# Two convolution stages of a fused image kernel run as one pipeline, dwc's convolution five blocks behind cpe1's

## Chip, cores and metric

The kernel runs on one core of a Trainium2 chip. The metric is the device time of one execution in microseconds (us), 3555.57 us as the median of three runs (3555.01 to 3556.33).

## What is computed

Four images of 128 channels by 96 x 96 go through four layers, all in float32 but the last convolution. The layers before and after (a patchwise filter, a selective scan, attention, an MLP, a binary convolution) are not touched. What the change moves is the head of the third layer:

```python
t = t + img2tok(_dwconv(tok2img(t), cpe1_w, cpe1_b))
shortcut = t
tn = _ln(t, n1_g, n1_b)
act_res = jax.nn.silu(tn @ actproj_w + actproj_b)
ti = tn @ inproj_w + inproj_b
ti = jax.nn.silu(img2tok(_dwconv(tok2img(ti), dwc_w, dwc_b)))
ta = _attn(ti, Hh, Ww, qk_w, qk_b, lepe_w, lepe_b)
```

`_dwconv` is a depthwise 3 x 3 convolution, `_ln` a normalisation over the 128 channels.

## The kernel before

Channels lie on the 128 partitions. An image is cut into NB = 12 blocks of 8 rows (768 columns), and each stage works block by block in one of four large regions `R[0]` to `R[3]`, with small double-buffered tiles in `work` and the eight banks of PSUM. Nothing is scheduled by a tool. For each engine the program writes out its instructions by `overlapped` (L71): a run is a start step and a list of (lag, stage), and at step t a stage of lag l in a run of start s is emitted for block t - s - l, in the order of the lists. Engines are joined by counting semaphores: `a.wait_ge(e1["var"], done(i, b))` waits for block b of image i. The order of a list is therefore the order of execution on its engine, and an instruction that waits holds up all behind it.

The head of the layer is two stages, one after the other, in `middle(i)` of each engine:

- **cpe1** (`cpe1_run`, start NB + 1, beside the last steps of the scan's normalisation `norm_run`). ScalarE writes the centre tap (`cpe1_centre`, L878), VectorE adds the left and right taps (`side_tap`, L1502), TensorE convolves the other six taps from row-shifted copies (`convolve`, L1128, by `shifted_taps`, L1033), VectorE adds the two (`add_taps`, L1487). Then the normalisation: TensorE subtracts the mean (`centre`), ScalarE squares (L865), TensorE averages (`var`), ScalarE takes Ln and Exp (`root`, L869, L871), VectorE multiplies (`normalise`, L1492). All products of TensorE go by `product` (L1013).
- **dwc** (`dwc_run`, start 2 NB + 4). TensorE multiplies by `w_in` and `w_act` (`in_act`, L1150), VectorE writes `ti` (L1513), ScalarE the Silu of the other (`silu_act`, L885). `dwc` convolves `ti` six blocks later in the same way (centre L896, taps L1502, sum L1520), and `silu_v` (L889) writes the result.

Then follow the keys of the attention (start 3 NB + 7): `stage` copies a block (L906), `keys` turns and multiplies it (L1176, L1177), `key_in` (L1533), `key_exp` (L914 to L918), `key_phi`, `key_turned` (L1548), `kv_sum` (L1193).

The row-shifted copies come by DRAM. SP's queue stores each finished block (`store_x` L554, `store_ti` L567) into a scratch, and fetches it in four DMAs (`fetch_shifted`, L536) into one of two halves of a buffer, `shifted_rows(p)`, p = b % 2, once the block after it has landed there and the convolution of block b - 2 is done. cpe1 and dwc both use both halves, dwc after cpe1:

```python
pipelined(sp, NB, [(3, load_x_shifted), (0, store_x)])
pipelined(sp, NB, [(3, load_ti_shifted), (0, store_ti)])
```

[...]

## Time and profile before

| | us |
|---|---|
| median of 3 runs | 3555.57 |
| profiled execution | 3555.76 |
| span of its trace | 3554.0 |
| TensorE busy | 2939.3 (83%) |
| VectorE busy | 2377.0 (67%) |
| ScalarE busy | 2255.9 (63%) |
| GpSimd busy | 1105.1 (31%) |

The span runs from the first to the last instruction. Busy shares are means over stages of different kinds, and say nothing of one stage. In a timeline a row is an instruction, or several of one line merged (x48), with its start, the time from its start to the end of the last, and in brackets the idle time of its engine before it with what ended it. Two instructions of one engine overlap at their ends by about 0.1 us. On TensorE a float32 matmul counts as two, so that a `product` of two halves is x4. [...]

### The profile page before, as it was taken

How to read it: one execution, taken by the hardware profiler on the slowest of the kernel's cores; microseconds unless marked ns; L12 is line 12 of the kernel's file. 1: busy time of each engine (PE TensorE's matmuls, PEld its weight loads, DVE VectorE, ACT ScalarE, POOL GpSimd, SP SyncE). 2: the span in 40 equal slices, each digit the busy share in tenths (PEclk: the TensorE clock that was granted, in tenths of full speed). 3: DMA queues.
4: the chain of work that ended last, by engine and by line, in shares of the span. 5: the costliest groups of instructions: out<-in, count | busy, mean ns of one | idle time of the engine just before them, and what ended most of it. 6: DMA issues, size and time to landing. Idle time of an engine off the chain costs nothing. (4 is left out here: it accounts for less than half of the span.)

```text
span 3554.0 us, 45053 instructions
## 1 busy us (share of the span) xinstructions
PE 2939.3 (83%) x17500; PEld 1601.4 (45%) x17500; DVE 2377.0 (67%) x2469; ACT 2255.9 (63%) x2485; POOL 1105.1 (31%) x612
## 2 busy tenths in 40 slices
PE   3688876979979877788997988777988788769799
PEld 2344335545535434444553543443555444354355
DVE  5777656875478646687457964768736876576861
ACT  2877545568687645447778774644868876454584
POOL 0246003642025500373103630146300462025530
...
GB/s 69 18 1 41 124 220 100 171 9 0 71 27 1 59 140 212 109 135 9 0 90 9 1 105 125 201 135 90 9 13 86 0 5 151 146 174 135 46 0 54
...
## 3 DMA queue, kind: packets, MB, share of 16 engines
...
q8 instruction: 141, 2.31, 0.3%
...
## 5 line engine op out<-in xcount | busy, mean ns | idle before, releaser
L1502 DVE SCALAR_TENSOR_TENSOR work<-region,cols,work 128x768 f32<-128x768 f32 x288 | 373.8, 1298 | 8.4 <-ACT work L896 3.3
L677 POOL TENSOR_TENSOR region<-region 128x768 f32<-128x768 f32 x96 | 230.9, 2407 | 322.2 <-ACT region L856 315.6
L1013 PE MATMUL psum<-region,m_fc 128*128 128x384 f32 x768 | 286.4, 496 | 11.1 <-ACT work L963 11.1
L1278 PE MATMUL psum<-work,m_fc 128*128 128x384 f32 x768 | 282.7, 492 | 0.0
L1013 PE MATMUL psum<-region,m_cen 128*128 128x384 f32 x384 | 162.6, 549 | 112.4 <-DVE region L1617 45.3
L220 DVE SCALAR_TENSOR_TENSOR region<-region,cols 128x768 f32<-128x768 f32 x192 | 239.8, 1249 | 4.0
L641 POOL TENSOR_TENSOR work<-work 128x768 f32<-128x768 f32 x48 | 99.4, 2074 | 439.8 <-ACT work L780 425.2
L653 POOL TENSOR_TENSOR work<-work,region 128x768 f32<-128x768 f32 x96 | 174.0, 1812 | 193.8 <-ACT work L795 193.8
L963 ACT ACTIVATE work<-psum,cols 128x768 f32<-128x768 f32 x192 | 173.0, 901 | 90.9 <-PE psum L1013 86.2
L1013 PE MATMUL psum<-work,m_avg 128*128 128x384 f32 x576 | 217.3, 500 | 15.1 <-ACT work L818 7.2
L1424 DVE SCALAR_TENSOR_TENSOR work<-region,cols,work 128x768 f32<-128x768 f32 x144 | 195.9, 1381 | 39.4 <-POOL work L641 36.0
L1013 PEld LDWEIGHTS psum<-region,m_fc 128*128 128x128 f32 x768 | 145.8, 194 | 123.5 <-ACT work L963 33.4
L692 POOL COPY region<-work 128x768 f32<-128x768 f32 x4 | 3.3, 826 | 634.9 <-DVE work L1539 634.9
L927 ACT ACTIVATE region<-psum,cols 128x768 f32<-128x768 f32 x48 | 43.2, 901 | 235.5 <-PE psum L1013 235.5
L1278 PEld LDWEIGHTS psum<-work,m_fc 128*128 128x128 f32 x768 | 142.9, 191 | 110.5 <-DVE region L1621 19.2
L1013 PEld LDWEIGHTS psum<-region,m_cen 128*128 128x128 f32 x384 | 70.2, 203 | 203.6 <-issue 113.8
L1445 DVE TENSOR_TENSOR_SCAN work<-work,psum 128x768 f32<-128x768 f32 x88 | 159.7, 1814 | 3.1
L1621 DVE SCALAR_TENSOR_TENSOR region<-psum,cols,region 128x768 f32<-128x768 f32 x48 | 48.9, 1018 | 165.8 <-PE psum L1278 165.8
L1013 PE MATMUL psum<-region,m_w_dt 128*128 128x384 f32 x384 | 146.3, 505 | 16.0 <-issue 10.3
L1013 PEld LDWEIGHTS psum<-work,m_avg 128*128 128x128 f32 x576 | 107.7, 193 | 108.8 <-ACT work L818 30.3
L704 POOL TENSOR_TENSOR region<-work,region 128x768 f32<-128x768 f32 x48 | 90.9, 1893 | 208.9 <-DVE work L1587 208.9
L669 POOL TENSOR_TENSOR region<-work,region 64x768 f32<-64x768 f32 x48 | 115.4, 2405 | 124.9 <-DVE work L1471 124.9
...
## 6 DMA issues: line engine op xcount, KB each, us to landing
...
```

The lines of the kernel that those rows point to most:

```text
L220: eng.scalar_tensor_tensor(out=tgt, in0=prow(k, b, *TAPS[n]), scalar=tap_weight(conv, TAPS[n]), in1=tgt, op0=ALU.mult, op1=ALU.add).then_i ...
L641: g.tensor_tensor(tile(4 + p), tile(p), tile(2 + p), ALU.add).then_inc(b_taps[0], 1)
L653: g.tensor_tensor(tile(2 + p), tile(p), flat(2, sweep_block(sweep, b)), ALU.mult).then_inc(c["du"], 1)
L669: g.tensor_tensor(flat(1, b)[0:CM], tile(2 + p)[CM:P], flat(1, b)[CM:P], ALU.mult).then_inc(d_gate, 1)
L677: g.tensor_tensor(chain_tile(conv, n, p), chain_tile(conv, n - 1, p), chain_tile(conv, n, p), ALU.add).then_inc(tap_done[n], 1)
L704: g.tensor_tensor(region_tile(3, 4 + p), tile(p), region_tile(3, 2 * p), ALU.mult).then_inc(f2_qc, 1)
L963: a.activation(halves(tile(4 + j)), pair(0), ACT.Gelu, bias=col("fc1_o", j)).then_inc(g_gelu, 1)
L1013: last = pe.matmul(psum[:, bank + s, 0:HC], weights[:, :], moving(s), start=(n == 0), stop=(n == len(terms) - 1))
L1278: last = pe.matmul(psum[:, 4 + s, 0:HC], fc2[:, P * j:P * (j + 1)], static(tile(4 + j))(s), start=(j == 0), stop=(j == 3))
L1424: v.scalar_tensor_tensor(out=by_row(tile(6 + p)) if n == 4 else sofar, in0=prow(3, b, *scan_tap(n)), scalar=col("l1taps", n), in1=sofar, o ...
L1445: v.tensor_tensor_scan(way(tile(6 + p)), way(tile(4 + p)), way(bu_flat[p]), initial=start, op0=ALU.mult, op1=ALU.add).then_inc(c["h"], 1)
L1502: v.scalar_tensor_tensor(out=by_row(tile(acc + p)), in0=prow(k, b, *TAPS[n]), scalar=tap_weight(conv, TAPS[n]), in1=by_row(tile(acc + p)), ...
```

## The change

cpe1 and dwc become one run, `local_run`, on each of the three engines. On TensorE it starts at NB + 1, on ScalarE and VectorE at NB + 2; dwc's convolution has lag 6 where cpe1's has 1. `in_act` is split into `to_in` and `to_act`, which use one pair of banks in turn. PSUM is shared out anew: cpe1's convolution and `var` in banks 0 and 1 (so `convolve` now waits for the Ln of the block before), `centre` in 2 and 3 without a second buffer, in and act in 4 and 5, dwc's convolution in 6 and 7. dwc's tiles move to `tile(4 + p)`. The keys' run starts at 2 NB + 3 on TensorE and 2 NB + 4 on the others. `root` and `silu_v` load their tables ahead of their waits. The two halves of the shifted rows are shared: cpe1 has both for its first five blocks (`FRESH`) and then half 0, dwc has half 1 and for its last four blocks both; a load into a half used alone waits for the convolution of block b - 1. SP's list is one, in which a load of dwc's last four blocks stands ahead of the store of its step and cpe1's load of block 2 ahead of the last store of cpe1.

```diff
 
...
 
+        def x_half(b):
+
+            return b % 2 if isinstance(b, int) and b < FRESH else 0
+
+        def ti_half(b):
+
+            return b % 2 if isinstance(b, int) and b >= NB - FRESH else 1
...
                 def load_x_shifted(b, p):
                     rows_landed(x_stored, b, p)
-                    sp.wait_ge(e1["conv"], done(i, b - 2))
-                    fetch_shifted("cpe1", b, p, x_shifted[p])
+                    sp.wait_ge(e1["conv"], done(i, b - 2 if b < FRESH else b - 1))
+                    fetch_shifted("cpe1", b, x_half(b), x_shifted[p])
...
                 def load_ti_shifted(b, p):
                     rows_landed(ti_stored, b, p)
-                    if is_first(b):
+                    if b == 0:
+                        sp.wait_ge(e1["conv"], done(i, FRESH - 2))
+                        sp.sem_inc(rows_seen, 1)
+                    if ti_half(b) == 0:
                         sp.wait_ge(e1["conv"], done(i, NB - 1))
-                        sp.sem_inc(rows_seen, 1)
-                    sp.wait_ge(e2_conv, done(i, b - 2))
-                    fetch_shifted("dwc", b, p, ti_shifted[p])
+                    sp.wait_ge(e2_conv, done(i, b - 2 if b > NB - FRESH else b - 1))
+                    fetch_shifted("dwc", b, ti_half(b), ti_shifted[p])
...
-                pipelined(sp, NB, [(3, load_x_shifted), (0, store_x)])
-                pipelined(sp, NB, [(3, load_ti_shifted), (0, store_ti)])
+                for b in range(NB):
+                    if b == NB - 1:
+                        load_x_shifted(2, 0)
+                    store_x(b, b % 2)
+                    if 3 <= b < 5:
+                        load_x_shifted(b - 3, (b - 3) % 2)
+                pipelined(sp, NB, [(0, lambda b, p: load_x_shifted(b, p) if 2 < b < FRESH else None),
+                                   (5, lambda b, p: load_ti_shifted(b, p) if b > NB - FRESH else None),
+                                   (3, store_ti),
+                                   (5, lambda b, p: load_ti_shifted(b, p) if b <= NB - FRESH else None),
+                                   (0, lambda b, p: load_x_shifted(b, p) if b >= FRESH else None)])
...
                 def root(b, p):
+                    a.preload_act_table_set("natural_log_exp_and_others")
                     a.wait_ge(e1["var"], done(i, b))
-                    a.activation(halves(tile(2 + p)), pair(6), ACT.Ln, bias=col("eps")).then_inc(e1["log"], 1)
...
-                cpe1_run = [(0, cpe1_centre), (3, squares), (4, root)]
...
                 def silu_act(b, p):
                     a.wait_ge(e2_mm, done(i, b))
-                    a.activation(halves(flat(2, b)), pair(2), ACT.Silu, bias=col("act_o")).then_inc(e2_act, 1)
+                    a.activation(halves(flat(2, b)), pair(4), ACT.Silu, bias=col("act_o")).then_inc(e2_act, 1)
 
                 def silu_v(b, p):
+                    a.preload_act_table_set("silu_and_others")
                     a.wait_ge(e2_sum, done(i, b))
-                    a.activation(prow(0, b), by_row(tile(2 + p)), ACT.Silu).then_inc(e2_v, 1)
...
                 def dwc_centre(b, p):
                     if is_first(b):
                         a.wait_ge(borders, i * 5 + 4)
                     a.wait_ge(e2_ti, done(i, b))
-                    a.wait_ge(e2_sum, done(i, b - 2))
-                    a.activation(by_row(tile(p)), prow(3, b), ACT.Identity, scale=tap_weight("dwc", TAPS[0]),
+                    a.wait_ge(e2_v, done(i, b - 2))
+                    a.activation(by_row(tile(4 + p)), prow(3, b), ACT.Identity, scale=tap_weight("dwc", TAPS[0]),
                                  bias=col("dwc_b")).then_inc(e2_centre, 1)
 
-                dwc_run = [(0, silu_act), (5, dwc_centre), (7, silu_v)]
+                local_run = [(2, squares), (0, cpe1_centre), (2, root), (6, silu_v), (5, dwc_centre), (3, silu_act)]
...
-                overlapped(a, NB, [(0, norm_run), (NB + 1, cpe1_run), (2 * NB + 4, dwc_run),
-                                   (3 * NB + 7, [(0, stage), (2, key_exp)])])
+                overlapped(a, NB, [(0, norm_run), (NB + 2, local_run), (2 * NB + 4, [(0, stage), (2, key_exp)])])
...
                     pe.wait_ge(e1["t"], done(i, b - 1))
+                    pe.wait_ge(e1["log"], done(i, b - 1))
...
-                    shifted_taps("cpe1", 0, p, True).then_inc(e1["conv"], 1)
+                    shifted_taps("cpe1", 0, x_half(b), True).then_inc(e1["conv"], 1)
...
                 def centre(b, p):
+                    if is_first(b):
+                        pe.wait_ge(d_norm, done(i, NB - 1))
                     pe.wait_ge(e1["t"], done(i, b))
-                    pe.wait_ge(e1["tn"], done(i, b - 2))
-                    product(2 + 2 * p, [(cen128, image_rows(1, b))]).then_inc(e1["yc"], 1)
+                    pe.wait_ge(e1["tn"], done(i, b - 1))
+                    product(2, [(cen128, image_rows(1, b))]).then_inc(e1["yc"], 1)
 
                 def var(b, p):
+                    pe.wait_ge(e1["sq"], done(i, b))
+                    product(0, [(avg128, static(tile(2 + p)))]).then_inc(e1["var"], 1)
+
+                def to_in(b, p):
+                    if is_first(b):
+                        pe.wait_ge(d_log, done(i, NB - 1))
+                    pe.wait_ge(e1["tn"], done(i, b))
+                    pe.wait_ge(e2_act, done(i, b - 1))
+                    product(4, [(w_in, flat_rows(2, b))]).then_inc(e2_in, 1)
+
+                def to_act(b, p):
+                    pe.wait_ge(e2_ti, done(i, b))
+                    product(4, [(w_act, flat_rows(2, b))]).then_inc(e2_mm, 1)
+
+                def dwc(b, p):
                     if is_first(b):
                         pe.wait_ge(d_out, done(i, NB - 1))
-                    pe.wait_ge(e1["sq"], done(i, b))
-                    pe.wait_ge(e1["log"], done(i, b - 1))
-                    product(6, [(avg128, static(tile(2 + p)))]).then_inc(e1["var"], 1)
-
-                cpe1_run = [(3, centre), (4, var), (1, convolve)]
-
-                def in_act(b, p):
-                    if isinstance(b, int) and b < 2:
-                        pe.wait_ge(e1["tn"], done(i, NB - 2 + b))
-                    pe.wait_ge(e2_ti, done(i, b - 1))
-                    pe.wait_ge(e2_act, done(i, b - 1))
-                    product(0, [(w_in, flat_rows(2, b))])
-                    product(2, [(w_act, flat_rows(2, b))]).then_inc(e2_mm, 1)
-
-                def dwc(b, p):
                     pe.wait_ge(ti_shifted[p], i * (32 * NB) + (b * 32 + (64 - 32 * p)))
-                    pe.wait_ge(e2_sum, done(i, b - 2))
+                    pe.wait_ge(e2_sum, done(i, b - 1))
                     pe.sem_inc(shift_begun, 1)
-                    shifted_taps("dwc", 4 + 2 * p, p, True).then_inc(e2_conv, 1)
-
-                dwc_run = [(0, in_act), (6, dwc)]
+                    shifted_taps("dwc", 6, ti_half(b), True).then_inc(e2_conv, 1)
+
...
```

VectorE's lists, which the cut leaves out, become `local_run = [(6, dwc_left), (6, dwc_right), (3, ti), (0, cpe1_left), (0, cpe1_right), (2, normalise), (6, dwc_sum), (1, cpe1_sum)]`, start NB + 2.

TensorE, the passage from cpe1 to dwc before (`m_cen` is centre, `m_avg` var, `m_w_in` and `m_w_act` in_act, `m_cpe_shifted` the convolution):

```order
L1033 MATMUL psum<-work,m_cpe_shifted 32x384 x24
L1013 MATMUL psum<-region,m_cen 128x384 x2
L1013 MATMUL psum<-work,m_avg 128x384 x2
L1013 MATMUL psum<-region,m_cen 128x384 x2
L1013 MATMUL psum<-work,m_avg 128x384 x4
L1013 MATMUL psum<-region,m_w_in 128x384 x2
L1013 MATMUL psum<-region,m_w_act 128x384 x2
```

and one full step of it now:

```order
L1034 MATMUL psum<-region,m_cen 128x384 x2
L1034 MATMUL psum<-region,m_w_in 128x384 x2
L1034 MATMUL psum<-work,m_avg 128x384 x2
L1054 MATMUL psum<-work,m_dwc_shifted 32x384 x24
L1054 MATMUL psum<-work,m_cpe_shifted 32x384 x24
L1034 MATMUL psum<-region,m_w_act 128x384 x2
```

All six kinds of work stand in one step, cpe1's convolution right behind dwc's.

ScalarE, the same passage before (L871 Exp, L885 silu_act, L896 dwc_centre, L889 silu_v):

```order
L871 ACTIVATE work<-work 128x768
L885 ACT_TABLE_LOAD
L885 ACTIVATE region<-psum,cols 128x768 x6
L896 ACTIVATE work<-region,cols 128x768
L885 ACTIVATE region<-psum,cols 128x768
L896 ACTIVATE work<-region,cols 128x768
L885 ACTIVATE region<-psum,cols 128x768
L896 ACTIVATE work<-region,cols 128x768
L889 ACTIVATE region<-work 128x8x96
```

and one full step now (L886 squares, L900 cpe1_centre, L891 Ln, L893 Exp, L911 silu_v, L918 dwc_centre, L906 silu_act):

```order
L886 ACTIVATE work<-psum 128x768
L900 ACTIVATE work<-region,cols 128x768
L889 ACT_TABLE_LOAD
L891 ACTIVATE work<-psum,cols 128x768
L893 ACTIVATE work<-work 128x768
L909 ACT_TABLE_LOAD
L911 ACTIVATE region<-work 128x8x96
L918 ACTIVATE work<-region,cols 128x768
L906 ACTIVATE region<-psum,cols 128x768
```

A table load that stood once between the stages now stands twice in each step.

TensorE at the end of dwc, before (L1176 and L1177 are `keys`):

```order
L1033 MATMUL psum<-work,m_dwc_shifted 32x384 x24
L1013 MATMUL psum<-region,m_w_in 128x384 x2
L1013 MATMUL psum<-region,m_w_act 128x384 x2
L1033 MATMUL psum<-work,m_dwc_shifted 32x384 x144
L1176 MATMUL psum<-m_w_k,region 128x128
L1177 MATMUL psum<-m_ident,region 128x128
```

and now (L1201 and L1202 are `keys`):

```order
L1034 MATMUL psum<-work,m_avg 128x384 x2
L1054 MATMUL psum<-work,m_dwc_shifted 32x384 x24
L1034 MATMUL psum<-region,m_w_act 128x384 x2
L1034 MATMUL psum<-region,m_w_in 128x384 x2
L1054 MATMUL psum<-work,m_dwc_shifted 32x384 x24
L1034 MATMUL psum<-region,m_w_act 128x384 x2
L1054 MATMUL psum<-work,m_dwc_shifted 32x384 x24
L1201 MATMUL psum<-m_w_k,region 128x128
L1202 MATMUL psum<-m_ident,region 128x128
```

The rest of in_act runs out beside blocks 7 and 8 of dwc's convolution, and `keys` of block 0 stands behind block 9, where it stood behind block 10.

## Rows read from the trace of the kernel before

**Rows 1.** Timeline of TensorE in cpe1: start us, us, engine, line, names, count, [idle before, releaser]

```profile
383.26 1.45 PE L1013 MATMUL psum<-work,m_avg 128*128 128x384 f32 x4
384.64 2.17 PE L1033 MATMUL psum<-work,m_cpe_shifted 64*32 64x384 f32 x48
387.66 1.53 PE L1013 MATMUL psum<-region,m_cen 128*128 128x384 f32 x4 [0.85 <-DVE region L1492]
```

**Rows 2.** Timeline of TensorE in dwc, where nothing is waited for

```profile
473.30 2.17 PE L1033 MATMUL psum<-work,m_dwc_shifted 64*32 64x384 f32 x48
475.40 1.56 PE L1013 MATMUL psum<-region,m_w_in 128*128 128x384 f32 x4
476.79 1.45 PE L1013 MATMUL psum<-region,m_w_act 128*128 128x384 f32 x4
```

**Rows 3.** Timeline of VectorE, key_in of block 3, image 0

```profile
540.93 0.94 DVE L1533 TENSOR_TENSOR work<-psum,m_kbias 128x768 f32<-128x768 f32 x1
```

**Rows 4.** Timeline of all engines, the chain of one normalisation

```profile
423.85 0.81 ACT L865 ACTIVATE work<-psum 128x768 f32<-128x768 f32 x1 [2.70 <-PE psum L1013]
...
425.14 0.90 ACT L869 ACTIVATE work<-psum,cols 128x768 f32<-128x768 f32 x1 [0.48 <-PE psum L1013]
...
426.08 0.84 ACT L871 ACTIVATE work<-work 128x768 f32<-128x768 f32 x1
...
426.95 0.95 DVE L1492 TENSOR_TENSOR region<-work,psum 128x768 f32<-128x768 f32 x1 [1.97 <-ACT work L871]
...
428.05 1.53 PE L1013 MATMUL psum<-region,m_cen 128*128 128x384 f32 x4 [0.85 <-DVE region L1492]
```

**Rows 5.** Timeline of all engines, a product and the VectorE instruction that reads it

```profile
451.21 1.45 PE L1013 MATMUL psum<-region,m_w_act 128*128 128x384 f32 x4
...
452.70 1.02 DVE L1513 TENSOR_SCALAR region<-psum,cols 128x768 f32<-128x768 f32 x1 [2.94 <-PE psum L1013]
```

**Rows 6.** Timeline of all engines, dwc's convolution and what follows it

```profile
496.31 2.17 PE L1033 MATMUL psum<-work,m_dwc_shifted 64*32 64x384 f32 x48 [1.35 <-DMA work<-scratch_dwc]
...
498.62 0.95 DVE L1520 TENSOR_TENSOR work<-work,psum 128x768 f32<-128x768 f32 x1 [0.56 <-PE psum L1033]
...
499.68 1.03 ACT L896 ACTIVATE work<-region,cols 128x768 f32<-128x768 f32 x1 [1.74 <-DVE work L1520]
500.61 0.83 ACT L889 ACTIVATE region<-work 128x768 f32<-128x768 f32 x1
```

**Rows 7.** Timeline of ScalarE in the scan, a table load between two activations

```profile
245.71 1.28 ACT L800 ACT_TABLE_LOAD   x1
247.00 1.76 ACT L805 ACTIVATE work<-work,cols 128x768 f32<-128x768 f32 x2
```

**Rows 8.** Timeline of all engines, the start of cpe1 in image 0

```profile
361.80 2.15 ACT L878 ACTIVATE work<-region,cols 128x768 f32<-128x768 f32 x2
...
367.32 0.94 DVE L1487 TENSOR_TENSOR region<-work,psum 128x768 f32<-128x768 f32 x1
...
367.55 2.90 PE L1013 MATMUL psum<-region,m_w_l1out 128*128 128x384 f32 x4 [3.20 <-DVE region L1477]
368.18 2.06 DVE L1502 SCALAR_TENSOR_TENSOR work<-region,cols,work 128x768 f32<-128x768 f32 x2
```

**Rows 9.** Timeline of the SP queue, the load of block 6, convolved at 496.31 (rows 6)

```profile
490.19 1.73 SPq L536 DMA_DIRECT2D work<-scratch_dwc  x4
```

**Rows 10.** Timeline of all engines, the slowest load of dwc rows and its convolution, image 3

```profile
3107.52 6.31 SPq L536 DMA_DIRECT2D work<-scratch_dwc  x8
...
3115.83 1.53 PE L1033 MATMUL psum<-work,m_dwc_shifted 64*32 64x384 f32 x16 [3.81 <-DMA work<-scratch_dwc]
```

**Rows 11.** Busy time by stretch: us, busy (instructions) per engine, clock, DMA share, GB/s

```profile
468.00:495.00 27.00, 26.96 (x330) 11.94 (x328) 20.68 (x22) 14.12 (x17) 0.00 (x0) 1.00 0.85 211
```

**Rows 12.** DMA issues in dwc's drain, the last store: KB, us to landing

```profile
scratch_dwc<-region SPq DMA_DIRECT2D x1, 490.0 KB, 6.0
```

**Rows 13.** Busy time of one stretch in dwc's drain, columns as in rows 11

```profile
503.70:506.90 3.20, 3.20 (x48) 1.24 (x40) 0.20 (x1) 0.00 (x0) 0.00 (x0) 0.50 0.60 193
```

62 lines of the change are left out of this document (32 added, 30 removed).

## Prediction, made before the changed kernel was run

> **What bounds it now.** I read the timeline of image 0 engine by engine, then the waits. In cpe1 a block costs TensorE a product `centre` and a product `var` (1.38 us each from start to start), a convolution of 2.17 and 0.85 idle: 5.78 us [rows 1]. That is a loop over three engines, not one full engine: centre, squares, var, Ln, Exp, normalise, and the next centre waits for normalise [rows 4]. dwc has two parts. Six blocks of in_act alone, then six with the convolution beside it, in which TensorE waits for nothing: 1.39 + 1.38 + 2.10 = 4.87 us a block [rows 1, 2]; and a drain in which the last six convolutions wait for loads (1.35 us at the first [rows 6]) and, after such waits, run at half the clock [rows 13]. From the first `cpe1_centre` at 361.80 [rows 8] to `key_in` of block 3 at 540.93 [rows 3], the point from which VectorE sets the pace of the keys, image 0 takes 179.1 us. Every image has this stretch once. TensorE's own work of a block is four products and two convolutions, 4 x 1.39 + 2 x 2.10 = **9.75 us** [rows 1, 2], so 117 us of the 179.
>
> **One full step after the change.** TensorE runs centre(b), in(b-1), var(b), dwc(b-4), convolve(b+1), act(b-1). With centre at 0: in 1.39, var 2.78, dwc 4.17, convolve 6.27, act 8.37, next centre 9.75. I check each wait against it.
> - ScalarE: squares 1.49 after centre, with 0.08 for the wait 1.57 [rows 5]; cpe1_centre 2.3 to 3.3 (1.03 long, the next starts 0.1 before its end [rows 6]); a table load of 1.28, from the end of one activation to the start of the next 1.29 [rows 7], so Ln at 4.6 (var alone would allow 2.78 + 1.49 = 4.27); Exp 0.94 later at 5.54, normalise 0.87 after that at 6.41 [rows 4]. The second load 6.4 to 7.7; silu_v at 8.3, dwc_centre 9.0, silu_act 9.9, end 10.8. The next in wants it at 9.75 + 1.39 = 11.14.
> - VectorE: two side taps of dwc to 2.3, ti at 1.39 + 1.49 = 2.9, two of cpe1 3.8 to 5.8, normalise 6.4, dwc_sum 7.3, cpe1_sum at 6.27 + 2.31 = 8.6 [rows 6]. It frees the next centre 1.10 later [rows 4], at 9.7. Margin 0.05: tight, but TensorE still sets the step.
> - SP issues the store of ti(b-1) at 4.0, dwc's load when dwc is done, 2.27 us after its start (the 2.17 of the row and 0.1 of handing over), 6.4 to 8.2, and cpe1's load behind it, 8.5 to 10.3. Each is wanted one step after, 7.5 us from its issue.
> - The two added table loads (2.6 us) are thus hidden beside TensorE's dwc and convolve; without that cover they would be seen (next part).
>
> **Fill.** TensorE's list is not shifted by the extra step, so convolve(0) stays beside l1_out(10). cpe1_sum(0) now stands behind the side taps of block 1: they take its place at 367.32, 1.98 us, so the sum is at 369.3 and centre(0) at 370.4, where l1_out(11) ends too [rows 8]: 8.6 us after 361.80. Four steps have no dwc in them. There var and convolve have nothing between them: convolve waits for Ln, 4.61 + 0.90 + 0.15 = 5.65, sum at 7.97, next centre at 9.1. The table load costs 0.34 us a step here. 4 x 9.1 = 36.4 us.
>
> **Middle.** Seven full steps, 7 x 9.75 = 68.3. Centre(11) is then at 8.6 + 36.4 + 68.3 = 113.3.
>
> **Drain**, counted from there. in(11) waits for silu_act(10), which stands behind a table load, silu_v(7) and dwc_centre(8): sum(7) 6.95, silu_v 7.94, silu_act 9.6, in(11) 10.64. dwc(8) 12.0, act(11) 14.1, dwc(9) 15.5, keys(0) behind `stage` at 18.8 to 20.9. dwc(10) is not set by an engine. ti(11) is written at 12.1, so store(11) goes out at 13.2; the late store needs 6.0 us to land [rows 12], then load(10) goes, and from a load's first issue to its convolution pass 496.31 - 490.19 = 6.1 us [rows 6, 9]: **25.3**. Then sum(10) 27.6, silu_v 28.6, dwc_centre, stage(2), Relu, table load, Exp(0) 33.2, key_phi(0) 34.05, key_in(1) 34.9, the second Exp, behind silu_v's and its own table load, 39.55, key_phi(1) 40.4, key_in(2) 41.3, key_turned(1) to 45.0, key_phi(2), key_in(3) at **45.9**. dwc(11) runs at 29.5 behind keys(1), its load is there, and hides. store(10) and load(9) (usable at 15.1) just make dwc(9).
>
> Sum: 113.3 + 45.9 = 159.2 against 179.1, a gain of 19.9 us. From it go:
> - **Clock.** [...] A restart at the low level loses half of some 3.3 us, 1.65. dwc(10) follows 4.4 us of idle: I take 1.4 of it on the chain. in(11) follows 3.0, the first fill step has gaps of 1.1 to 1.8: a third of 1.65 each, 1.1. Bounds: 0 (none falls) and 9.7 (each of the four fill steps, in(11) and dwc(10) pay it).
> - **Loads.** In the full steps each stream has one half of the buffer, so a load can go only when the block before is convolved, 2.27 us after that starts, and the step is at least 2.27 + L, L being issue to use. At 6.1 that is 8.4, hidden; the slowest of the trace, 3115.83 - 3107.52 = 8.3 [rows 10], gives 10.57, 0.82 more, 5.7 over seven steps. Bounds 0 and 5.7; bandwidth allows it (two loads and a store, 1960 KB a step, at 211 GB/s for a share of 0.85, or 248 full [rows 11], are 7.9 us). The low end is nearer, since 6.1 was seen with the queue as full as it will be: 0.3.
> - The order of SP's list in the fill, the semaphores of the side taps, one more increment a block: nothing. The first loads are wanted 9 us and more after they can go, and SP sits in waits for most of a step; if that cover were gone, a load would come late by its place in the list, 1.7 us (rival 2 holds that).
>
> Net 19.9 - 2.5 - 0.3 = 17.1 us an image, over four images 68. The profiled execution took 3555.76 us (span 3554.0), the median is 3555.57, so the difference is nothing to this sum: 3555.6 - 68 = **3488 us**. Own range 3478 to 3503: a step of 10.0 instead of 9.75 would cost 7.
>
> **Rivals.**
> 1. *Nothing is given back.* No restart is slow on the chain: 19.9 x 4 = 80, 3476 us. For: 0.85 and 1.1 us of idle cost no clock today. Against: rows 8.
> 2. *The loads set the step.* Both streams are fetched within 2 us of each other through one half each; with L at 8.3 in every step +23, 3511 us. For: DMA is busy 0.85 of the time already at 211 GB/s [rows 11]. Against: convolutions without a wait at that share.
> 3. *The clock.* The fill's gaps of 1.5 us put each of its steps at the low level, and in(11) too: 9.7 - 2.5 = 7.2 more an image, 3517 us.
> 4. *ScalarE becomes the bound, and the kernel is slower.* The two table loads of a step stand in the chain. Were one to hold the engine for twice what rows 7 show, 2.57 us, Ln would come at 5.9, the second load end at 10.3, silu_act start at 11.9 and in at 12.94, a step of 11.55: 7 x 1.8 = 12.6, the fill 4 x 1.28 = 5.1, the drain's four loads about 4, together 21.7 against the 17.1 gained: +18, 3574 us. It decides from 2.3 us a load. Against it: rows 7, where Exp starts 0.01 us behind the load and the load stands right behind the activation before. [...]
> 5. *It doesn't overlap.* A wait that I take for met is not, and a step keeps the old sum, 5.78 + 4.87 = 10.65 us: +25, 3513 us.
>
> **Chances.** Forecast 0.50, rival 1 0.14, rival 2 0.14, rival 3 0.10, rival 4 0.05, rival 5 0.04, and 0.03 for losses together that end within 0.2% of today (7 us, what a measurement of this kernel can tell from no change). Faster are the forecast and rivals 1, 2, 3, 5: 0.92; same 0.03; slower 0.05. The range 3470 to 3525 takes in rivals 1, 2, 3 and 5 and their near neighbours, leaving out rival 4 and sums of several losses.
>
> **What would show it.** In the changed profile: centres 9.1 us apart four times, then 9.75 seven times, with TensorE idle under 0.2 us in each of these; two table loads of 1.28 us a step; key_in(3) about 162 us after the first cpe1_centre; dwc(10) released by a DMA some 25 us after centre(11), with the clock at 0.5 behind it; waits of SP for cpe1's and dwc's convolutions, not the other way. Wrong would be: TensorE released by loads in the full steps (rival 2), by ScalarE with table loads before it (4), by VectorE's cpe1_sum at more than 9.9 us apart (the margin of 0.05 was none), or a fill at 0.5 clock (3).

## The result, and the profile after

| | before | after |
|---|---|---|
| median, us | 3555.95 (4 runs, 3555.01 to 3557.17) | 3458.80 (4 runs, 3457.40 to 3462.03) |
| span of the trace, us | 3554.0 | 3456.1 |
| c0 to key_in(3), us, image 0 | 179.1 | 158.0 |
| c0 to the first query_phi, us, images 0 to 3 | 237.5, 240.8, 236.6, 237.5 | 216.4, 215.6, 215.4, 216.7 |
| first query_phi to first x3 addition of the MLP, us | 165.0, 164.9, 160.3, 165.0 | 160.2, 160.6, 160.5, 165.2 |

Here c0 is the start of the first `cpe1_centre` of an image, and each length is the difference of two starts in the timeline. The ratio is 0.9728, 95% interval 0.9711 to 0.9745: 97 us faster, where 68 was forecast, and below the range of 3470 to 3525. The kernel goes the way that the prediction says; it goes further. Run again later beside each other, the two kernels took 3562.0 and 3461.0, a difference of 101.

The page of the changed kernel, part 1. TensorE is busy 32 us less for the same 17500 instructions, ScalarE 127 us more for 100 table loads more.

```profile
PE 2907.3 (84%) x17500; PEld 1593.0 (46%) x17500; DVE 2381.8 (69%) x2469; ACT 2382.6 (69%) x2585; POOL 1107.3 (32%) x612
```

One full step in image 0, timeline of TensorE (start us, length us, engine, line of the changed kernel, names; in brackets the idle time before and what ended it). It answers to [rows 1, 2]: the six pieces of the forecast in their order, 10.07 and 10.15 us from `m_cen` to `m_cen`.

```profile
440.38 2.17 PE L1054 MATMUL psum<-work,m_dwc_shifted 64*32 64x384 f32 x48
442.85 2.17 PE L1054 MATMUL psum<-work,m_cpe_shifted 64*32 64x384 f32 x48 [0.30 <-DMA work<-scratch_cpe]
444.95 1.56 PE L1034 MATMUL psum<-region,m_w_act 128*128 128x384 f32 x4
446.34 1.46 PE L1034 MATMUL psum<-region,m_cen 128*128 128x384 f32 x4
447.64 1.48 PE L1034 MATMUL psum<-region,m_w_in 128*128 128x384 f32 x4
448.95 1.46 PE L1034 MATMUL psum<-work,m_avg 128*128 128x384 f32 x4
450.34 2.17 PE L1054 MATMUL psum<-work,m_dwc_shifted 64*32 64x384 f32 x48
453.00 2.17 PE L1054 MATMUL psum<-work,m_cpe_shifted 64*32 64x384 f32 x48 [0.49 <-DMA work<-scratch_cpe]
455.10 1.56 PE L1034 MATMUL psum<-region,m_w_act 128*128 128x384 f32 x4
456.49 1.46 PE L1034 MATMUL psum<-region,m_cen 128*128 128x384 f32 x4
```

Eleven steps from centre(0) to centre(11) in that image: 9.22, 9.13, 9.03, 9.03 without dwc, then 9.42, 9.75, 9.52, 10.07, 10.15, 9.75, 10.25. In the shortest nothing waits, and the pieces are a little shorter than reckoned: `in` and `var` come 1.30 and 1.32 behind the product before them, and the two convolutions take 1.96 and 2.07. The steps above 10 carry a wait for cpe1's load, 0.30, 0.49 and 0.60; over four images 9 of the 28 full steps have such a wait. That load goes out behind dwc's, SP queue of the same stretch:

```profile
442.65 1.73 SPq L546 DMA_DIRECT2D work<-scratch_dwc  x4
445.11 2.63 SPq L546 DMA_DIRECT2D work<-scratch_cpe  x4
```

Issued at 445.11 and used at 453.00, 7.9 us; the one before took 6.9 (435.97 to 442.85). By the forecast's own bound, 2.27 + L, the step is then 10.16, and it took 10.15: loads and TensorE are within half a microsecond of each other.

ScalarE in that step: the load stands right behind `cpe1_centre`, Ln follows it 1.29 after its start, and so 4.53 after centre at 436.27; Exp, VectorE's normalise and the second load follow, as in [rows 4] with [rows 7] put in. Ln and Exp run behind the one load; silu_v, dwc_centre, silu_act and the next block's squares and cpe1_centre run behind the other, with no load until 449.58.

```profile
438.47 1.02 ACT L900 ACTIVATE work<-region,cols 128x768 f32<-128x768 f32 x1
...
439.51 1.28 ACT L889 ACT_TABLE_LOAD   x1
...
440.80 0.90 ACT L891 ACTIVATE work<-psum,cols 128x768 f32<-128x768 f32 x1
441.74 0.84 ACT L893 ACTIVATE work<-work 128x768 f32<-128x768 f32 x1
442.60 1.28 ACT L909 ACT_TABLE_LOAD   x1
442.61 0.95 DVE L1516 TENSOR_TENSOR region<-work,psum 128x768 f32<-128x768 f32 x1 [0.42 <-ACT work L893]
```

The drain, timeline of all engines from in(11) to the last key_in that counts, centre(11) at 476.49. It answers to [rows 3, 6, 9, 12]:

```profile
486.94 2.18 PE L1034 MATMUL psum<-region,m_w_in 128*128 128x384 f32 x4 [2.81 <-ACT region L906]
489.06 3.13 PE L1054 MATMUL psum<-work,m_dwc_shifted 64*32 64x384 f32 x48
489.17 1.02 DVE L1535 TENSOR_SCALAR region<-psum,cols 128x768 f32<-128x768 f32 x1 [1.05 <-PE psum L1034]
490.21 0.34 SPq L577 DMA_DIRECT2D scratch_dwc<-region  x1
...
493.00 4.68 SPq L546 DMA_DIRECT2D work<-scratch_dwc  x8
...
499.97 2.17 PE L1054 MATMUL psum<-work,m_dwc_shifted 64*32 64x384 f32 x48 [0.86 <-DMA work<-scratch_dwc]
...
520.59 0.94 DVE L1554 TENSOR_TENSOR work<-psum,m_kbias 128x768 f32<-128x768 f32 x1
```

The store of ti(11) goes out at 490.21 and the load that waits for its landing at 493.00: 2.8 us, where the forecast took 6.0 from [rows 12]. In the other images this takes 3.3, 2.7 and 2.7 us. dwc(10) comes 7.0 behind that load's issue; load(11) is issued beside it, but that this is what slows it was not tested. In images 1 and 2 dwc(10) does not wait for its load, and key_in(3) comes 21.3 and 21.4 behind it instead of 20.6: there another wait ends last. And the start of the fill in two images, timeline of TensorE: the same work, the same 3.20 us of idle before it, and the work behind it is at the low clock for 2.8 us in image 2 and for 5.7 in image 3 (the granted clock reads 0.50, where 1.00 is full, from 2054.4 to 2057.8 and from 2894.1 to 2900.9).

```profile
2054.97 2.90 PE L1034 MATMUL psum<-region,m_w_l1out 128*128 128x384 f32 x4 [3.21 <-DVE region L1501]
2057.77 1.55 PE L1034 MATMUL psum<-region,m_cen 128*128 128x384 f32 x4
```

```profile
2894.72 2.90 PE L1034 MATMUL psum<-region,m_w_l1out 128*128 128x384 f32 x4 [3.20 <-DVE region L1501]
2897.51 2.90 PE L1034 MATMUL psum<-region,m_cen 128*128 128x384 f32 x4
```

Where the difference of the two profiles is, 97.8 us: 88.3 between c0 and the first query_phi (21.2, 25.1, 21.1, 20.9), 8.7 between query_phi and x3, 0.9 in the rest. So two questions stand: what the stretch gained beyond 17.1 an image, and whether the other 9 belong to the change at all.

### The profile page after: what moved, and what is told of

It is laid out like the page before. It is cut to its first block and busy times, and to the rows that moved or that the text cites. A ratio compares the mean times of both kernels' runs of the same rounds, so it can differ in the third digit from the quotient of the medians.

```text
span 3456.1 us, 45158 instructions
## 1 busy us (share of the span) xinstructions
PE 2907.3 (84%) x17500; PEld 1593.0 (46%) x17500; DVE 2381.8 (69%) x2469; ACT 2382.6 (69%) x2585; POOL 1107.3 (32%) x612
## 5 line engine op out<-in xcount | busy, mean ns | idle before, releaser
L1034 PE MATMUL psum<-region,m_fc 128*128 128x384 f32 x768 | 286.5, 497 | 10.7 <-ACT work L984 10.7
L984 ACT ACTIVATE work<-psum,cols 128x768 f32<-128x768 f32 x192 | 172.9, 900 | 90.6 <-PE psum L1034 85.8
L1034 PE MATMUL psum<-region,m_cen 128*128 128x384 f32 x384 | 159.8, 542 | 73.7 <-DVE region L1638 41.9
L948 ACT ACTIVATE region<-psum,cols 128x768 f32<-128x768 f32 x48 | 43.2, 900 | 229.6 <-PE psum L1034 229.6
L816 ACT ACTIVATE work<-psum,cols 128x768 f32<-128x768 f32 x96 | 86.4, 900 | 95.9 <-PE psum L1034 95.7
```

The costliest lines, as they stand in the source:

```text
L984: a.activation(halves(tile(4 + j)), pair(0), ACT.Gelu, bias=col("fc1_o", j)).then_inc(g_gelu, 1)
L1034: last = pe.matmul(psum[:, bank + s, 0:HC], weights[:, :], moving(s), start=(n == 0), stop=(n == len(terms) - 1))
```

## Experiments

Each run is set beside the changed kernel, 3458.8 us, or where it ran beside its control, 3461.0. A length of an image is again a difference of starts.

**The price of a table load.** Every load of cpe1 and dwc doubled:

```diff
 def root(b, p):
+    a.preload_act_table_set("silu_and_others")
     a.preload_act_table_set("natural_log_exp_and_others")
 def silu_v(b, p):
+    a.preload_act_table_set("natural_log_exp_and_others")
     a.preload_act_table_set("silu_and_others")
```

> The changed kernel with every table load of cpe1 and dwc doubled (the other set is loaded first), so that a switch holds ScalarE 2.57 us where it held 1.28. Results are the same. My theory (the prediction's step model with rival 4's numbers): Ln at 5.9 instead of 4.6, the second pair ends at 10.3, silu_act at 11.9, the next in 1.39 + 9.75 cannot be kept and a full step becomes 11.55; a fill step becomes 10.4; together about 21.7 us more an image, 3459 + 87 = 3546 us. Rival A (table loads lie beside other work with much slack, so that doubling them is hidden in the full steps too): only the fill pays, 4 x 1.28 x 4 = 20, 3480 us. Rival B (a load drains the engine as well, more than its own 1.28 us): above 3570 us.

Measured 3535.5 us (3533.5 to 3536.5), 77 more. Fill steps 10.31 to 10.42 (10.4 expected) but for the first of each image, 11.65 to 12.17; full steps 11.14, not 11.55; the drain 48.3 us instead of 44. Busy time of one such step, columns as in [rows 11]:

```profile
447.46:458.60 11.14, 10.03 (x114) 4.53 (x113) 7.68 (x8) 11.04 (x12) 0.00 (x0) 1.00 0.73 170
```

ScalarE is full: four loads at 1.28 and seven activations (squares, centre, Ln, Exp, silu_v, dwc_centre, silu_act), each followed by the next after 0.7 to 1.0, are the 11.14, and TensorE and VectorE wait for it. A pair of loads costs 2.58 us from the first start to the next activation, with nothing behind it: 440.33 and 441.62 the loads, 442.91 Ln. The same run is rival 4 made real. With one load a switch, as the change has it, ScalarE needs 8.6 of the 9.75, an estimate: 11.14 less two loads.

**Its place.** The load of Ln behind the wait for var:

```diff
 def root(b, p):
-    a.preload_act_table_set("natural_log_exp_and_others")
     a.wait_ge(e1["var"], done(i, b))
+    a.preload_act_table_set("natural_log_exp_and_others")
```

> The changed kernel with the table load of Ln issued behind the wait for var instead of ahead of it, so that it cannot run in the time in which ScalarE waits. My theory (the load is on the chain only by its place): in the fill Ln moves from 4.6 to 4.27 + 1.29 = 5.56 after centre, a fill step from 9.1 to 10.05; in a full step normalise goes to 7.4, dwc_sum, silu_v, dwc_centre and silu_act slide behind it until in waits for silu_act, a step of about 10.6 (0.8 more). 4 x 0.95 + 7 x 0.8 = 9.4 us an image, about 3497 us. Rival (ScalarE has slack in the full steps): only the fill pays, 4 x 0.95 x 4 = 15, 3474 us.

Measured 3509.2 us (3506.4 to 3516.5), 50 more; full steps 10.49 (10.6 expected), fill steps 9.88 and 9.96 (10.05), but in each image the first at 11.07 and one more at 11.46 to 11.49, with TensorE at half its clock, in the first after the 3.2 us of idle ahead of l1_out(11), in the other after one of 2.3 us. All in all centre(11) comes 10.1 us later than in the changed kernel, where 9.4 were expected. The 12 us beyond the expectation lie mostly behind it: the drain takes 46.7 to 46.9 us instead of 44, 11 us over four images, and the expectation had nothing there. The load is cheap in the change because it stands in front of a wait.

**Five blocks behind, or four.**

```diff
-local_run = [(2, centre), (3, to_in), (2, var), (6, dwc), (1, convolve), (3, to_act)]
+local_run = [(2, centre), (3, to_in), (2, var), (5, dwc), (1, convolve), (3, to_act)]
-                   (5, lambda b, p: load_ti_shifted(b, p) if b > NB - FRESH else None),
                    (3, store_ti),
-                   (5, lambda b, p: load_ti_shifted(b, p) if b <= NB - FRESH else None),
+                   (4, load_ti_shifted),
```

(with dwc's stages of VectorE and ScalarE and the keys one turn earlier too)

> The changed kernel with dwc's convolution, side taps, sum and silu_v one step earlier (four blocks behind cpe1's convolution of the same turn instead of five), loads of dwc behind the store of their turn. My theory (TensorE sets the full step, and the last dwc blocks wait for the last store and load, not for their turn): one fill step becomes a full step, +0.65 us an image; dwc's load goes out 6.9 us after the centre before and is wanted 13.9 after it, which a load of 6.1 to 7.0 just makes. Nothing gained in the drain, since the chain ti(11), store, load, dwc(10) is as long as before: 3459 + 3 = 3462 us, at most 3475 if loads come late by up to 0.5 us a step. Rival (the lag of five sets the length of the drain): a step less in the drain, 9.75 - 0.65 = 9 us an image, 3423 us. Rival (loads then set the step, 8.3 us from issue to use as the slowest of the trace before): +1.3 us a step, 3500 us.

Measured 3493.2 us (3486.5 to 3500.5), 34 more. The drain is as long as before, 42.9 to 44.7 us from centre(11) to key_in(3), so the lag does not set it: that part of the theory held. The margin of the loads did not: full steps of 9.9 to 11.8. TensorE in one of 11.79, both convolutions waiting, and ahead of it the SP queue:

```profile
426.04 0.34 SPq L577 DMA_DIRECT2D scratch_dwc<-region  x1
431.13 1.73 SPq L546 DMA_DIRECT2D work<-scratch_dwc  x4
432.97 1.78 SPq L546 DMA_DIRECT2D work<-scratch_cpe  x4
...
437.09 2.17 PE L1053 MATMUL psum<-work,m_dwc_shifted 64*32 64x384 f32 x48 [0.46 <-DMA work<-scratch_dwc]
440.86 2.17 PE L1053 MATMUL psum<-work,m_cpe_shifted 64*32 64x384 f32 x48 [1.60 <-DMA work<-scratch_cpe]
```

The theory's 3462 to 3475 missed, and its rival with the loads, 3500, is nearest: a full step is 10.7 on average, 0.9 more, where that rival had 1.3. The cause is not the length of the loads alone. Four blocks behind, dwc's load needs the rows of the store of its own turn. That store, issued at 426.04, lands after 5.0 us, and the load goes 0.08 us behind, at 431.13, where the convolution (426.17) would have let it go at 428.44; cpe1's load stands behind it in SP's list, goes at 432.97 and is used at 440.86. The theory had dwc's load going 6.9 us after the centre; here it goes 9.0. In the changed kernel dwc's load goes 2.27 us behind the start of its convolution, 0.6 to 2.0 us before the store of its turn has landed, whose rows it does not need. So the fifth block hides the landing of the store.

**Late stores first**, as an order of SP would be without the change's exception (store_x(11) before load_x(2), store_ti before the load in the late turns).

```diff
+                    store_x(b, b % 2)
                     if b == NB - 1:
                         load_x_shifted(2, 0)
-                    store_x(b, b % 2)
-                   (5, lambda b, p: load_ti_shifted(b, p) if b > NB - FRESH else None),
                    (3, store_ti),
-                   (5, lambda b, p: load_ti_shifted(b, p) if b <= NB - FRESH else None),
+                   (5, load_ti_shifted),
```

> The changed kernel with SP's list in the other order where the change put loads ahead of late stores: store_x(11) before load_x_shifted(2), and store_ti before dwc's load in each late turn. My theory: load(9) of dwc then waits for ti(11) and goes at 13.7 after centre(11) instead of 10, next to load(10), so dwc(9) comes 3 us later and dwc(10) 1 to 2 us; in the fill nothing, because block 2's convolution is wanted much later: 3459 + 6 = 3465 us. Rival (the order is what makes the drain short): a whole load more on the chain, 6 us an image, 3483 us. Rival (hidden): 3459 us.

Measured 3479.1 us (3476.8 to 3485.0), 20 more, between theory and rival. The drain takes 47.1 to 48.6 us instead of 43.8 to 44.1; the fill is the same. load(9) and load(10) now go out together at 493.97, and dwc(9) pays for both, idle and clock:

```profile
501.23 3.71 PE L1053 MATMUL psum<-work,m_dwc_shifted 64*32 64x384 f32 x48 [4.33 <-DMA work<-scratch_dwc]
```

**Without the extra step** of VectorE and ScalarE (NB + 2 to NB + 1, 2 NB + 4 to 2 NB + 3).

> The changed kernel with the parts of ScalarE and VectorE for cpe1, dwc and the keys one turn earlier (NB + 1 and 2 NB + 3), as TensorE's are; only how they interleave with the last turns of the normalisation before changes. My theory (the extra step lets the last residuals and gates of that normalisation go first, on which l1_out(11) and centre(0) hang): without it cpe1_centre(0) starts earlier, but the residuals wait behind cpe1's side taps, and the point that counts, centre(0), comes no earlier; between 0 and 2 us an image lost, 3461 to 3469 us. Rival (the extra step is a step of delay for the fill): 2 to 9 us an image gained, 3450 us or less. Rival (nothing hangs on it): 3461 us.

Measured 3479.5 us (3475.9 to 3487.0), 18 to 21 more than the changed kernel. centre(0) comes 13.5 to 15.2 us after c0 instead of 8.55, key_in(3) 161.4 to 164.3 instead of 157.1 to 158.3. l1_out(11) now waits 6.04 us for the residual of block 10, which stands behind side taps of cpe1 on VectorE:

```profile
366.17 2.07 DVE L1525 SCALAR_TENSOR_TENSOR work<-region,cols,work 128x768 f32<-128x768 f32 x2 [4.09 <-ACT work L900]
368.16 1.14 DVE L1501 SCALAR_TENSOR_TENSOR region<-psum,cols,region 128x384 f32<-128x384 f32 x2
369.44 2.90 PE L1034 MATMUL psum<-region,m_w_l1out 128*128 128x384 f32 x4 [6.04 <-DVE region L1501]
```

So the step of delay is worth about 5 us an image: it lets the end of the work before go first. The expectation had this mechanism, but at 0 to 2 us an image.

**What sets the drain.** First one move on ScalarE:

```diff
+def silu_act_early(b, p):
+    if b == 10:
+        a.preload_act_table_set("silu_and_others")
+        silu_act(b, p)
-local_run = [(2, squares), (0, cpe1_centre), (2, root), (6, silu_v), (5, dwc_centre), (3, silu_act)]
+local_run = [(2, squares), (0, cpe1_centre), (2, root), (3, silu_act_early), (6, silu_v),
+             (5, dwc_centre), (3, lambda b, p: silu_act(b, p) if b != 10 else None)]
```

(silu_v(7) then loads no table of its own)

> The changed kernel with one move on ScalarE, in the drain: silu_act(10) stands ahead of silu_v(7) and dwc_centre(8), behind the same table load. Before it, in(11) waited 2.81 us for silu_act. My theory (the chain of the drain runs silu_act(10), in(11), ti(11), store, load, dwc(10)): in(11) at 8.6 after centre(11) instead of 10.45, the rest as before, 1.8 us an image, or 2.5 if TensorE's clock stays high through the shorter wait: 3459 - 7 = 3452, down to 3449 us. Rival (the drain is set by dwc's sums and silu_v): no change, 3459 us, or later by the 0.9 us that silu_v slides, 3462 us.

Measured 3463.2 us (3460.4 to 3465.8): nothing gained. in(11) did come at 8.73 after centre(11) (10.45 before), but ti(11) only at 12.25 (12.68), because on VectorE it stands behind the side taps of block 8, which wait for ScalarE:

```profile
486.44 2.07 DVE L1532 SCALAR_TENSOR_TENSOR work<-region,cols,work 128x768 f32<-128x768 f32 x2 [2.54 <-ACT work L924]
488.43 1.01 DVE L1542 TENSOR_SCALAR region<-psum,cols 128x768 f32<-128x768 f32 x1
```

My theory had left out the queue of the engine behind the one that I freed. In the changed kernel run again, further down, in(11) ran at full clock and ti(11) came at 12.02 without any move. Of silu_first's own drains two took 42.7 us and two 45, the latter with dwc(10) at half the clock (3.80 and 3.71 us). So the next run moves `ti(11)` too:

```diff
-local_run = [(6, dwc_left), (6, dwc_right), (3, ti), (0, cpe1_left), (0, cpe1_right), (2, normalise),
+local_run = [(3, lambda b, p: ti(b, p) if b == NB - 1 else None), (6, dwc_left), (6, dwc_right),
+             (3, lambda b, p: ti(b, p) if b < NB - 1 else None), (0, cpe1_left), (0, cpe1_right), (2, normalise),
```

> The changed kernel with silu_act(10) ahead of silu_v(7), as before, and in the same turn ti(11) ahead of the side taps of dwc's block 8 on VectorE. The first move alone brought in(11) from 10.45 to 8.73 us after centre(11), but ti(11) only from 12.68 to 12.25, because it stands behind the side taps (486.44 to 488.43). My theory (VectorE's order sets the drain): ti(11) at 10.2, its store and the last loads 2 us earlier, dwc(10) at about 21 instead of 22.5 to 23.5, key_in(3) at 41 after centre(11): 2.5 us an image less than the changed kernel, 3461 - 10 = 3451 us. Rival (the last loads or sum(9) set dwc(10) whenever ti(11) is written): 3459 us.

Measured 3452.0 us (3450.9 to 3461.1); the control, the changed kernel run again beside three others, gave 3461.0. The drain takes 41.4 to 42.5 us, where the control's profile has 42.3 to 43.1. ti(11) is at 10.30 after centre(11), and dwc(10) is still released by its load in three images of four:

```profile
489.80 1.02 DVE L1542 TENSOR_SCALAR region<-psum,cols 128x768 f32<-128x768 f32 x1 [2.57 <-PE psum L1041]
490.74 2.06 DVE L1532 SCALAR_TENSOR_TENSOR work<-region,cols,work 128x768 f32<-128x768 f32 x2
...
501.37 2.17 PE L1061 MATMUL psum<-work,m_dwc_shifted 64*32 64x384 f32 x48 [1.82 <-DMA work<-scratch_dwc]
```

Where its load releases it, in all images of the control and in three here, key_in(3) comes 20.6 us behind dwc(10): the chain of the forecast (silu_act, in, ti, store, load, dwc(10)) with VectorE's order added sets the end there. In the fourth image dwc(10) waits for nothing at 19.98, and key_in(3) comes 21.4 behind it. The total is near the expected 3451, but in part by luck: the drain gives 0.9 us an image, 3.4 in all, and not 10. Between the two profiles 3 us more lie ahead of centre(11), most of it in first fill steps at full clock, and 7.5 between query_phi and x3, which the edit does not touch.

**The fill's bank.** In the fill the convolution waits for Ln, because var and it share PSUM pair 0.

```diff
-    product(0, [(avg128, static(tile(2 + p)))]).then_inc(e1["var"], 1)
+    product(6 if b < 4 else 0, [(avg128, static(tile(2 + p)))]).then_inc(e1["var"], 1)
```

(Ln reads that pair, the convolutions behind blocks 0 to 3 no longer wait for Ln, dwc(0) waits for Ln of block 3)

> The changed kernel with var of blocks 0 to 3 in the PSUM pair 6, which dwc does not use yet, so that the next convolution need not wait for Ln to have read var. My theory (in the fill the convolution waits for Ln at 5.65; without that it starts at 4.2 and the next centre is set by normalise and the sum behind it on VectorE): a fill step of 8.4 instead of 9.1, 4 x 0.7 = 2.8 us an image, 3459 - 11 = 3448 us. Rival (the fill is set by Exp and normalise or by loads, not by the convolution): 3459 us.

Measured 3457.0 us (3450.3 to 3459.1), 2 to 4 of the 11 us, and its runs overlap the changed kernel's. The later fill steps are 8.32 (8.4 expected), but the first two 9.7 and 9.55 in three images of four; there centre(0) and centre(1) run at half the clock, centre(1) after 2.14 us of idle. Image 2, where they don't, has 8.41 and 8.32, and centre(11) 110.84 us after c0 against 113.5. The mechanism is right, and the clock takes most of the gain back; with the clock held it arrives (warm_both below).

**Is it the clock, and whose?** Two kernels with a pause of 1.4 us between keys and attention, by copies whose output is not used:

```diff
+v.tensor_copy(region_tile(3, 9)[:, 3 * P:6 * P], psum[:, 7, 0:3 * P])
+v.tensor_copy(halves(region_tile(3, 11)), pair(4))
 v.tensor_copy(region_tile(3, 9)[:, 0:2 * P], psum[:, 7, 0:2 * P])
```

> The kernel before with two copies more on VectorE (384 and 768 columns, about 1.4 us together) in the chain between the keys and the attention of each image; their output is not used. From the first query_phi to the first addition of the MLP the kernel before took 165.0 us in three images and 160.3 in one, the changed one 160.2 to 160.6 in three and 165.2 in one. My theory (the difference is TensorE's clock at two restarts and falls by when the restart comes, not by the work): the pause costs 4 x 1.4 = 5.6 us, and some images change from 165 to 160 or back, so that the total is off from 3556 + 5.6 by a multiple of about 4.7 us. Rival (the 165 belongs to what the old order leaves behind in queues or buffers): all images keep their 165.0, 165.0, 160.3, 165.0 and the total is 3561.5 us.

> The changed kernel with the same two copies at the same place. My theory: as there, each image takes about 160.4 or 165.1 us from the first query_phi to the first addition of the MLP, and which one changes with the shift; total 3459 + 5.6 give or take a multiple of 4.7 us. Rival (the change itself makes this part short): three images of 160.2 to 160.6 and one of 165.2 as before, 3464.5 us.

Before with the pause: 3561.1 us (the kernel before beside it 3558.3), query_phi to x3 now 160.6, 162.9, 162.9, 163.0, where it was 165.0, 164.9, 160.3, 165.0. After with the pause: 3471.8 us, and 164.5, 160.6, 164.6, 164.7, where it was 160.2, 160.6, 160.5, 165.2; the four together are 8 us longer, which with the 5.6 of the pauses is the 13 measured. Before's total alone would fit the rival, 3561.5; the images decide. They change sides in both kernels, and there is a level near 163 that I had not expected. The control shows the same without any edit:

> The changed kernel itself again, as the control for the three runs beside it: 3459 us, within the 3457 to 3462 of its first four runs. From the first query_phi to the first addition of the MLP each image falls on about 160.4, 162.9 or 165 us; if the theory of the clock by its moment is right, not in the same images as in the first profile (160.2, 160.6, 160.5, 165.2).

Measured 3461.0 us (3458.1 to 3463.6), with 165.1, 163.0, 162.2, 162.9, and the first fill step 10.36 in all four images. Then the clock was held, by products of constants in the waits:

```diff
+def keep_warm(bank, times):
+    for _ in range(times):
+        product(bank, [(cen128, lambda s: fc1[:, 0:HC])])
...
...
+    if isinstance(b, int) and b == NB - 1:
+        pe.wait_ge(d_log, done(i, b))
+        keep_warm(4, 2)
     pe.wait_ge(d_gate, done(i, b))
```

(the second piece in l1_out; in in(11) the same with `keep_warm(0, 1)` ahead of its wait for silu_act)

> The changed kernel with products of constants, written to PSUM pairs that nothing uses at that moment, in two waits of TensorE per image: two ahead of l1_out(11), where it is idle for 3.2 us and then runs at half its clock, and one ahead of in(11) in the drain (2.81 us idle). My theory (the clock falls because of these waits, and how long it stays low varies by 3 us from image to image for the same work): l1_out(11) takes 1.5 instead of 2.90 us, the first fill step is 9.0 in all four images (9.22, 9.15, 9.02 and 10.37 in the first profile), in(11) 1.5 instead of 2.18: 0.3 to 1.4 and 0.7 us, together some 4 to 6 us over four images, 3454 us. Rival (a low clock costs nothing on this chain): 3459 us. Rival (the added products delay what waits behind them): 3463 us.

Measured 3457.5 us (3454.5 to 3460.8), 3.5 less, interval not clear of the control's. The first fill step is 9.00 or 9.01 in all four images.

> The same with products of constants also ahead of query(1), attend(0), g_centre(2) and g_centre(3), the four waits of 2.9 to 4.2 us at the start of the attention and of the MLP. My theory: the stretch from the first query_phi to the first addition of the MLP comes in every image below the fastest seen so far, 160.2 us, since no profile has had both restarts at full clock: about 158, some 14 us less than the changed kernel beyond what the local products give: 3441 us. Rival (the modes are no matter of the clock): the four images go on falling on 160 to 165, 3455 us.

Measured 3438.1 us (3436.1 to 3443.0), 23 less than the control. query_phi to x3 is 157.1, 157.5, 157.5, 157.5. TensorE at the restart of the MLP, in the changed kernel (image 3) and in this one (image 0):

```profile
3263.82 2.90 PE L1034 MATMUL psum<-region,m_cen 128*128 128x384 f32 x4 [3.98 <-DVE region L1638]
```

```profile
726.43 2.74 PE L1034 MATMUL psum<-m_fc,m_cen 128*128 128x384 f32 x8
730.25 1.53 PE L1034 MATMUL psum<-region,m_cen 128*128 128x384 f32 x4 [1.07 <-DVE region L1655]
```

The added products are the `x8` row; the wait behind them is 1.07 us and the product that counts runs at full clock. The clock was held at those waits alone: at the start of the MLP, 114 to 139 us behind query_phi, it still reads 0.50 for 17 to 21 us an image. And the pair ahead of g_centre(3) stands where there was next to nothing to fill; image 0 of the changed kernel, then of this one:

```profile
748.64 1.53 PE L1034 MATMUL psum<-region,m_cen 128*128 128x384 f32 x4 [0.36 <-DVE region L1638]
```

```profile
743.32 2.74 PE L1034 MATMUL psum<-m_fc,m_cen 128*128 128x384 f32 x8
745.90 1.45 PE L1034 MATMUL psum<-region,m_cen 128*128 128x384 f32 x4
```

From the first x3 to the second it is 15.57 us in all images of all kernels with these products, and 13.59 or 13.60 without them. So 2.0 us an image are given back just behind the stretch that I measured (in the last image they reach the end of the kernel, 187.3 us behind the first x3 instead of 185.3); the 23 us are what is left. A kernel without that pair was not run. Last, the same in the kernel before:

> The kernel before with the products of constants ahead of query(1), attend(0), g_centre(2) and g_centre(3) and nothing else. It is to tell whether what came outside the changed stretch (8.6 us of 97 between the first query_phi and the first addition of the MLP) belongs to the change. My theory (it is TensorE's clock at those restarts, and falls to either kernel by chance): this stretch takes 157.1 to 157.6 us in all four images here too, where the kernel before took 165.0, 164.9, 160.3, 165.0: 26 us less, 3530 us; and the run with all products, 3438, is then 92 us below its own partner, 88 of the stretch and 3 to 4 of the local products. Rival (the new order lets the attention start better, through queues or buffers): 160 to 165 us in this kernel even with the clock held, 3545 us and more.

Measured 3542.4 us (3537.9 to 3543.8; the kernel before beside it 3563.6), and query_phi to x3 157.2, 157.6, 157.1, 157.5, as in the changed kernel. That settles it: with the clock held at its restarts the stretch behind the first query is the same in both, so the 8.7 us there belong to the clock and not to the order. That they fall by the moment at which the restarts come rests on the two runs with the pause. The totals gave less than I expected (21 of 26 us), and the two orders with the clock held differ by 104 us, not 92. In their profiles 93 of the 100 are between c0 and query_phi (the products ahead of l1_out(11) and in(11) are in the changed kernel alone), 4 before the first c0 and 3 between x3 and the next c0, parts in which no clock was held.

**Both moves and the clock held.** The best kernel is the changed one with var's bank, silu_act(10) early and the products of constants but the one ahead of in(11), and on top of that ti(11) early and one product ahead of dwc(10).

> The moves of the earlier runs together: var of blocks 0 to 3 in PSUM pair 6, silu_act(10) ahead of silu_v(7), and the products of constants except the one ahead of in(11). With the clock held in the fill, the first two fill steps of the other bank, which took 9.7 and 9.55 in three images of four, take 8.4 and 8.3, so that centre(11) comes 3 us earlier in every image; the drain is 1.2 us shorter where the clock stays high. 4 x (3 + 1.2) = 17 us less than the run with all products: 3424 us. Rival (the bank's gain is taken by later steps, which loads then set): 3437 us.

> The control for the next: 3430 us as before, within 3427 to 3435.

> The run with both moves and the products of constants, with ti(11) ahead of the side taps of block 8 as well and one product of constants ahead of dwc(10), which ran at half the clock (3.80 us) where the wait for its load was long. My theory: key_in(3) at 40.5 us after centre(11) instead of 42.6, in every image: 8 us less than the control, 3422 us. Rival (the moved ti delays the sum of block 8 and with it dwc(9) by as much): 3430 us.

Measured 3430.1, again 3427.6, and with ti 3421.5 us (3419.4 to 3430.3), ratio to the kernel before 0.9611 (0.9592 to 0.9631). Of the 17 us that were expected below the run with all products, 3438.1, 8.0 and 10.5 came. Fill steps 8.32 to 8.35 in every image, and centre(11) at 110.4 to 111.1 where the products alone have 113.0 to 114.1: with the clock held the bank's gain of 3 us an image arrives. The 1.2 of the early silu_act does not: the drain takes 42.6 to 43.6, with the products alone 42.3 to 43.2. With ti early the drain takes 41.9 us from centre(11) to key_in(3) in all four images (42.7 to 42.9 in the control): 1 of the 2 us expected. dwc(10) stands at 21.27 after centre(11) in all four, right behind the product added ahead of it, so that product now sets it. The runs of the last two overlap. c0 to key_in(3) is 152.3 to 152.8 us.

## Why the prediction was wrong

Its mechanism was right and its sum too small: 68 us forecast, 97 measured. Two terms were mis-sized most: in the drain the landing of the late store, 6.0 us forecast and 2.8 measured, and the 2.5 us taken off for the clock, of which image 0 paid 0.9. Together with the smaller terms below they are 4 us an image, 16 of the 29 missing; 4 come from image 1 and 9 from the clock outside the stretch.

- **What bounds it, and one full step.** Held on average: 68.9 us for seven steps against 68.3. In part that is luck, since single steps take 9.42 to 10.25: pieces shorter than reckoned make up for waits for cpe1's load of up to 0.6, where the forecast allowed 0.2 of idle. In place are Ln at 4.53 against 4.6, squares, Exp, normalise and the second load. VectorE's margin of 0.05 was enough.
- **Fill.** Held to the tenth in image 0: centre(0) at 8.55 (8.6), four steps 36.4 (36.4). That convolve waits for Ln is shown by var_bank (8.32 without it), and the table load's place by load_behind_var. That centre(0) comes so early is the extra step: without it 5 us later, by no_late_step.
- **Drain.** 44.1 against 45.9. The term that was mis-sized is "the late store needs 6.0 us to land": 2.8 measured. The store that I took it from was issued right behind a load, and the one now goes alone. Other stores fit this: right behind a load one took 7.0 in the kernel before (496.90), and 2.8 and 3.1 us behind the last DMA of one 3.7 and 3.0 in the new one (470.09, 480.35). It was not tested by a run, and four_behind has 5.0 us at such a distance. The load behind it took 7.0, not 6.1. With in(11) 0.2 earlier than forecast but at half the clock, ti(11) came 0.5 later; 0.5 - 3.2 + 0.9 is the 1.8. From dwc(10) on the forecast's chain fits to 0.1: key_in(1) 9.6 behind, key_in(3) 20.6. Its cause for in(11), silu_act, was right, but in(11) alone sets nothing; VectorE's order comes right behind (silu_first, ti_first).
- **"From it go" clock 2.5 and loads 0.3.** The other step that failed. In image 0 the loads took 0.6, and of the clock's 2.5 only 0.2 in the first fill step and 0.7 in in(11) are on the chain. dwc(10) came with 0.86 us of idle and at full clock, where I charged 1.4. What the clock did take is already in the fill and drain measured, so the 2.8 charged here come back whole: 2.8 + 1.8 - 0.6 = 4.0, against the 4.1 us between 17.1 and image 0's 21.2. The 1.65 us for a restart, from which the 2.5 and the bound of 9.7 are reckoned, was my estimate, and no run shows it as the price of one. The clock did read 0.50 for 3.4 us in the drain of the kernel before (503.52 to 506.92, of which [rows 13] has 3.2), but for 3.4 and 6.8 us in images 2 and 3 at the fill shown above, a part of it in idle time. In the changed kernel's four images in(11) took 2.18, 1.75, 1.85 and 2.90 us, where 1.53 is its time at full clock (490.42 in after_again), and the first fill step lost 0.2, 0.1, 0.0 and 1.4 us against the 9.0 with the clock held (warm_local).
- **Image 0 for all.** Image 1 took 182.4 us to key_in(3) before, not 179.1: 1.5 us came before centre(0), where the granted clock stayed at 0.50 longer, and 1.7 behind centre(11). With 0.7 less in the new order it won 4 us more. Over three profiles of either kernel with this code (before, before with the pause, before with the clock held behind it) the old order took 178 to 183 us, 180.2 on average; the new one 157.1 to 158.6, 157.7 on average. So the gain is 22.5 us an image, 90 in all. The new order also has fewer long waits in which the clock can fall; that this is why it varies less was not tested.
- **Outside the stretch.** The forecast had nothing there. 8.7 us came, and they belong to no order: see before_warm. Twelve images of the changed code average 162.8 us from query_phi to x3, eight of the code before 163.1.
- **Rivals.** 1 (nothing given back, 3476) was nearest and would still have missed. 2 happens in 9 of 28 full steps, by 0.2 to 0.6 us (7.9 us of load in a step that allows 7.5), not by 0.8 in each. 3 happens, by 1.35 us in the first fill step of some images and by 0.2 to 1.4 in in(11) of the first profile's, not in the later fill steps. 4 was priced well in the total: at twice the load 77 us are lost where the rival says 87 (a full step of 11.14, not 11.55), and one load costs 1.29 as the row had it. Two loads in a row cost 2.58 us, both of them together. 5 fell.

Open: why the kernel before, with the clock held at the four restarts, is 104 us behind the changed one with the clock held and not 90 to 93. In the profiles the rest lies before the first c0 (361 to 366 us in both kernels) and between x3 and the next c0 (464 to 469), where both vary from image to image.
